# TensorE's semaphore waits placed anew in a single-core cross-attention and gated-adapter kernel

## The chip, the core and the metric

One core of one Trainium2 chip runs the whole kernel. The time is the device time of one execution in microseconds (us); the median of three runs of the kernel before is 473.6 us (472.96 to 475.18). Each engine has its own stream of instructions; they meet only at semaphores. An instruction of this program carries at most one wait of its own. Where the source asks for more, the first stays on the instruction (for a product: on its weight load) and the others go into a separate instruction ahead of it, which the profile shows as EVENT_SEMAPHORE on "PEldq", TensorE's sequencer.

## The reference, cut to what matters

Four sequences of 512 tokens of 1024 features; 64 context rows each.

```
x = x + tanh(g0) * attention(layernorm(x), ctx)
    Q = rmsnorm(text @ Wq.T + bq); K = rmsnorm(rmsnorm(ctx) @ Wk.T + bk)
    attended = softmax(Q @ K.T / sqrt(1024)) @ rmsnorm(ctx)
x = x + tanh(g1) * ffn(layernorm(x))
    base = x @ W_base.T + b_base
    w    = normalised, thresholded softmax gate over 8 experts
    out  = base + 2 * sum_e w_e * (x @ A_e.T) @ B_e.T
```

All of it is float32. The kernel splits an operand into a high and a low part and makes one exact product from three fast ones: high*high, high*low, low*high.

## The kernel before, in words

Each engine's function walks the same list `stages` (lines 355 to 480), written out by hand, and issues what belongs to it; the list is the order of the work.

**First part (to about 240 us).** Q is never formed. With the Gram matrix of Wq (stage `g`) a block of 512 tokens needs only y = G x, in eight column blocks j (stage `y`, lines 674 to 688, one PSUM bank each, three products for each row r in `ROWS[j]`; column block 0 has one row, so three products in all), and its scores s = M x (stage `s`, line 689). VectorE turns each y bank into squares, GpSimd adds them. While block b is in `y`, the block before it is finished: `tops` (transposes of scores, after y(b,0)), `norms` (transposes of the norm sums, after y(b,1)), `pt` (transposes of the probabilities, after s(b)) and `attend` (after y(b,4) to y(b,7), two pairs of products, each emptied by VectorE in line 1465).

**Second part.** Token tiles go in pairs p = 0..7. Pair 0 takes the plain eight 512x128 block products, pairs 1 to 7 seven products P1, P2, P6, P5, P7, P3, P4 (a Winograd scheme; `PRODUCTS`, line 302) over sums of token blocks and of weight blocks (T1 to T4). Each is 12 instructions (lines 769, 771, 773: four k, three high/low products) and adds into PSUM bank A, B, C or D. VectorE adds bank A into the output rows after P1, P6 and P7 and bank C after P5 (stage `part`, line 1534, counted by `v_ev`); P6 may not touch bank A before P1 was read out. In front of the seven come `hd` (the gate and the adapter's A, banks 4 and 5), after P1 and P2 or P6 the one transpose `mt`, after P5 the transposes `zt` a21 and a22 of the next pair, after P7 a11, after P3 a12; `fin` adds the adapter's B. In pair 0 some of this stands elsewhere.

**The ring.** Transposes and `attend` share PSUM banks 7 and 6 in turn. `ring_open` (line 520) gives the next bank and waits until the entry two before it was emptied, by ScalarE (`a_ring`) or VectorE (`v_ring`). `tokens_ready` (line 533) waits for a token block's low part. All of `tensor` (line 519) is in the order of the list, so a wait that isn't met holds everything behind it.

Of the kernel before, what the change touches and what calls it, by code (L numbers as in the profile page):

```python
# [43 lines left out]
def build(nc, x, xt, ctx, front, wq, wk, wb, hd, bt, vec, fn_w, b_base, scal, out):  # L44
    T, D = x.shape
    S_ALL = ctx.shape[0]
    KB = D // P
# [22 lines left out]
    with ExitStack() as stack:  # L70
# [179 lines left out]

        SWEPT = [sorted((min(row, c), max(row, c)) for _, pieces in sweep for row, cols, _ in pieces for c in cols) for sweep in SWEEPS]
# [85 lines left out]
        for p in range(NP):  # L337
            for name, *_ in products(p):
                prod_no[p, name] = len(prod_no) + 1
                if name in PARTS and not plain(p):  # L340
                    ev_no[p, name] = len(ev_no) + 1
            for b_, _, _ in whole(p):
                ev_no[p, b_] = len(ev_no) + 1
        last_use = {op: max(prod_no[p, n] for p in range(NP) for n, _, o, _, _ in products(p) if o == op) for op in w_at}
# [174 lines left out]
        def tensor(pe):  # L519
            def ring_open(key, engine, split=False):  # L520
                n = ring.add(key, engine, split)
                if n >= 2:
                    engine, count = ring.empty(n - 2)
                    pe.wait_ge(ring_sem[engine], count)
                return bank[T_BANKS[n % 2]]
# [21 lines left out]
            for stage, *i in stages:  # L547
# [5 lines left out]
                elif stage == "mr":  # L553
                    b, = i
                    pe.wait_ge(g_mr, b + 1)
                    if b == 0:
                        pe.wait_ge(v_gl, 4)
                    else:
                        pe.wait_ge(v_z, 4 * b)
# [4 lines left out]
                elif stage == "zt":  # L564
# [17 lines left out]
                    acc = ring_open((stage, p, name), "act" if copied else "dve", split=not copied)  # L582
                    pe.wait_ge(a_xn, seq[2 * p + j] + 1)
                    transposes(acc, src)
                elif stage == "mt":
                    t, = i
                    acc = ring_open((stage, t), "dve", split=True)
                    pe.wait_ge(v_mm, t + 1)
                    transposes(acc, mm[t % 2][:, :].unsqueeze(1))
                elif stage == "pt":  # L590
                    b, = i
                    acc = ring_open((stage, b), "act")
# [81 lines left out]
                elif stage == "y":  # L674
# [7 lines left out]
                    pe.wait_ge(v_zl, 4 * b + max(ROWS[j]) // CK + 1)  # L682
                    for r in ROWS[j]:
                        g = block_no(r, j)
                        pe.matmul(acc[:, :], gram[:, g, 0, :], xth[b % 2][:, r, :], start=r == ROWS[j][0], stop=False)  # L685
                        pe.matmul(acc[:, :], gram[:, g, 1, :], xth[b % 2][:, r, :], start=False, stop=False)  # L686
                        done = pe.matmul(acc[:, :], gram[:, g, 0, :], xtl[b % 2][:, r, :], start=False, stop=r == ROWS[j][-1])  # L687
                    done.then_inc(p_y, 1)
                elif stage == "s":
                    b, = i  # L690
                    acc = bank[S_BANKS[b % 2]]
                    pe.wait_ge(v_zl, 4 * b + 4)
                    if b == 0:
                        pe.wait_ge(v_ml, KB)
                    elif b > 1:
                        pe.wait_ge(a_st, b - 1)
                    for r in range(KB):
                        pe.matmul(acc[:, :], mk[:, r, b, :], xth[b % 2][:, r, :], start=r == 0, stop=False)
                        done = pe.matmul(acc[:, :], mk[:, r, b, :], xtl[b % 2][:, r, :], start=False, stop=r == KB - 1)
                    done.then_inc(p_s, 1)  # L700
                elif stage == "norms":
                    b, = i
                    acc = ring_open((stage, b), "dve")
                    pe.wait_ge(g_qsum, qsums(b, FB - 1))
                    transposes(acc, sq_sum[:, :].rearrange("p (j t) -> p j t", j=TPB))
                elif stage == "tops":
                    b, = i
                    acc = ring_open(("weights", b), "dve")
                    pe.wait_ge(a_st, b + 1)
                    transposes(acc, st_sb[:, :].rearrange("p (j t) -> p j t", j=TPB))  # L710
                elif stage == "attend":
                    t, = i
                    b = t // TPB
                    for h in range(NH):
                        acc = ring_open((stage, t, h), "dve")
                        if t % TPB == 0 and h == 0:
                            engine, count = ring.empty(ring.number["pt", b])
                            pe.wait_ge(ring_sem[engine], count)
                            pe.wait_ge(v_fn, b + 1)
                        cols = half(h)  # L720
                        pe.matmul(acc[:, :], pt[b // 3][:, t % TPB, :], fnh[:, cols], start=True, stop=False)
                        pe.matmul(acc[:, :], pt[b // 3][:, t % TPB, :], fnl[:, cols], start=False,
                                  stop=True).then_inc(p_ring, 1)
                elif stage == "hd":
                    p, j = i
                    acc = bank[H_BANKS[j]]
                    if p > 0:
                        pe.wait_ge(v_hg, 2 * p - 1 + j)
                    elif j == 0:
                        pe.wait_ge(v_hw, 3)  # L730
                        pe.wait_ge(v_first, 3)
                    else:
                        pe.wait_ge(a_st, B)
# [4 lines left out]
                    for n, (name, w) in enumerate(uses):  # L738
                        tokens_ready(p, name)
                        z = z_slot[p, name]  # L740
                        for k in range(KH):
                            pe.matmul(acc[:, 0:2 * HEAD], zh[z][:, k, :], hw[w][:, k, :], start=n == k == 0, stop=False,  # L742
                                      skip_group_check=True)
                            done = pe.matmul(acc[:, 0:HEAD], zl[z][:, k, :], hw[w][:, k, 0:HEAD], start=False,  # L744
                                             stop=n == 1 and k == KH - 1, skip_group_check=True)
                    done.then_inc(p_hd, 1)
                elif stage == "prod":
                    p, n = i
                    name, tok, op, n_bank, opens = products(p)[n]
                    if opens and p == 0:  # L750
                        pe.wait_ge(*{"A": (v_dot, NQ - 2), "B": (v_dot, NQ - 1), "C": (v_first, 4), "D": (v_dot, NQ)}[n_bank])
# [5 lines left out]
                    if op in WHOLE_KEPT:  # L757
                        pe.wait_ge(v_wl, SPLITS[op, 1])
                    else:
                        pe.wait_ge(ld_w[op], T_BACK[op])  # L760
                    z = z_slot[p, tok]
                    parts = [(C_BANK[n_bank], 0, HALF)]
                    if (p, name) == (NP - 1, "P4"):
                        parts = spans(p, 3)
                        pe.wait_ge(v_hg, NT - 1)
# [905 lines left out]
```

## Time and profile before

| | |
|---|---|
| median of 3 runs | 473.6 us (472.96 to 475.18) |
| profiled execution: time and span | 473.6 us, with nothing outside the span that matters |
| TensorE products / weight loads, busy | 468.0 us (99%) / 399.3 us (84%) |
| VectorE, ScalarE, GpSimd busy | 361.7 us (76%), 173.8 us (37%), 119.8 us (25%) |
| granted TensorE clock | full in all 40 slices |
| share of the last chain | TensorE 78%, VectorE 8%, DMA 8% |

Products overlap in the pipeline: a 128x512 product shows as 0.39 us long, but the next begins 0.23 us after it. What is to be read is therefore the distance between the starts, not the length. The weight load of a product begins when the product before it begins.

### The profile page before, as it was taken

How to read it: one execution, taken by the hardware profiler on the slowest of the kernel's cores; microseconds unless marked ns; L12 is line 12 of the kernel's file. 1: busy time of each engine (PE TensorE's matmuls, PEld its weight loads, DVE VectorE, ACT ScalarE, POOL GpSimd, SP SyncE). 2: the span in 40 equal slices, each digit the busy share in tenths (PEclk: the TensorE clock that was granted, in tenths of full speed). 3: DMA queues.
4: the chain of work that ended last, by engine and by line, in shares of the span. 5: the costliest groups of instructions: out<-in, count | busy, mean ns of one | idle time of the engine just before them, and what ended most of it. 6: DMA issues, size and time to landing. Idle time of an engine off the chain costs nothing.

```text
span 473.6 us, 6945 instructions
## 1 busy us (share of the span) xinstructions
PE 468.0 (99%) x2481; PEld 399.3 (84%) x2481; DVE 361.7 (76%) x750; ACT 173.8 (37%) x349; POOL 119.8 (25%) x107
## 2 busy tenths in 40 slices
PE   8999999999999999999999999999999999999997
PEld 7898999998887888888888888878888888888886
DVE  1687996588888978879987888968777678877733
ACT  5847532332224305226334625342241421414300
POOL 0020511002344253345242406031230502205000
PEclk9999999999999999999999999999999999999999
DMA  8993129958576378576379640221405032050202
GB/s 320 412 408 118 76 90 389 405 183 286 197 246 248 133 252 283 193 292 229 141 273 419 277 144 36 81 98 46 133 1 175 4 89 90 2 177 1 89 1 89
DMA packets 22114, 84.40 MB, mean 178 GB/s; under 512 B 2624, under 2 KB 3904, under 8 KB 19264
## 3 DMA queue, kind: packets, MB, share of 16 engines
q1 hardware_dynamic: 21792, 83.81, 48.2%
q8 instruction: 20, 0.33, 0.3%
q10 hardware_dynamic: 288, 0.15, 0.1%
q14 instruction: 14, 0.11, 0.1%
HBM read 61.93 MB, written 22.02 MB: 177 GB/s over the span
## 4 chain that ended last, share of the span: by engine, by line
PE 78%; DVE 8%; DMA 8%; issue 3%; ACT 1%; POOL 1%; SPq 0%; DVEq 0%; ACTq 0%
PE bank L769 10%; PE bank L773 10%; PE bank L771 10%; PE bank L649 6%; PE bank L685 5%; PE bank L687 5%; PE bank L686 5%; PE bank L530 4%; PE bank L742 4%; DMA xst<-x_dram 3%; DMA T_low<-t_low_T 2%; DMA xz<-xt_dram 2%; DMA out_dram<-xs 2%; PE bank L599 2%; DVE wl_B L1438 1%
## 5 line engine op out<-in xcount | busy, mean ns | idle before, releaser
L1554 POOL TENSOR_TENSOR small<-small,tiny 128x1 f32<-128x1 f32 (+2 forms) x25 | 23.6, 942 | 167.1 <-DVE small L1183 137.9
L1534 DVE SCALAR_TENSOR_TENSOR xs<-bank,tiny,xs 128x512 f32<-128x512 f32 (+1 forms) x61 | 43.3, 739 | 20.6 <-PE bank L773 14.9
L685 PE MATMUL bank<-xth,gram 128*128 128x512 f32 x144 | 57.3, 398 | 0.0
L687 PE MATMUL bank<-xtl,gram 128*128 128x512 f32 x144 | 56.3, 391 | 0.0
L686 PE MATMUL bank<-xth,gram 128*128 128x512 f32 x144 | 56.1, 390 | 0.0
L769 PE MATMUL bank<-wh_B,zh 128*128 128x512 f32 x116 | 47.0, 405 | 0.1
L769 PE MATMUL bank<-wh_T,zh 128*128 128x512 f32 (+1 forms) x116 | 46.6, 402 | 0.0
L1582 POOL TENSOR_TENSOR sq_sum<-sq_sum,sq 128x512 f32<-128x512 f32 x24 | 32.0, 1333 | 56.5 <-DVE sq L1362 56.5
L773 PE MATMUL bank<-wh_B,zl 128*128 128x512 f32 x116 | 45.6, 393 | 0.0
L771 PE MATMUL bank<-wl_B,zh 128*128 128x512 f32 x116 | 45.4, 391 | 0.0
L773 PE MATMUL bank<-wh_T,zl 128*128 128x512 f32 (+1 forms) x116 | 44.7, 386 | 0.0
L771 PE MATMUL bank<-wl_T,zh 128*128 128x512 f32 (+1 forms) x116 | 44.6, 385 | 0.0
L1614 POOL TENSOR_TENSOR xs<-xs,bb 128x1024 f32<-128x1024 f32 x16 | 39.3, 2461 | 10.3 <-ACT zn L1022 7.7
L1362 DVE SCALAR_TENSOR_TENSOR sq<-bank,gsm,xz 128x512 f32<-128x512 f32 x32 | 23.8, 746 | 14.1 <-PE bank L687 12.6
L979 ACT ACTIVATE xth<-xz 128x1024 fp32r<-128x1024 f32 x16 | 17.0, 1061 | 42.3 <-DVE xz L1258 42.3
L687 PEld LDWEIGHTS bank<-xtl,gram 128*128 128x128 f32 x144 | 27.0, 188 | 5.9
L686 PEld LDWEIGHTS bank<-xth,gram 128*128 128x128 f32 x144 | 27.1, 188 | 5.3
L685 PEld LDWEIGHTS bank<-xth,gram 128*128 128x128 f32 x144 | 27.1, 188 | 5.2
L742 PE MATMUL bank<-hw,zh 128*128 128x276 f32 x128 | 31.1, 334 | 0.0
L744 PE MATMUL bank<-hw,zl 128*128 128x138 f32 x128 | 29.0, 227 | 0.0
L1022 ACT ACTIVATE zn<-xs,small 128x1024 f32<-128x1024 f32 x16 | 19.9, 1242 | 24.1 <-POOL small L1606 24.1
L1047 ACT ACTIVATE zh<-zr 128x512 fp32r<-128x512 f32 x28 | 17.5, 633 | 24.7 <-DVE zr L1298 10.5
(200 smaller groups left out, 1133.2 us busy)
## 6 DMA issues: line engine op xcount, KB each, us to landing
xst<-x_dram SPq DMA_DIRECT2D x16, 512.0 KB, 4.4
xz<-xt_dram SPq DMA_DIRECT2D x16, 512.0 KB, 7.6
out_dram<-xs SPq DMA_DIRECT2D x14, 512.0 KB, 2.7
xa<-x_dram SPq DMA_DIRECT2D x12, 512.0 KB, 3.4
x<-xa SPq DMA_DIRECT2D x12, 512.0 KB, 3.0
xs<-x SPq DMA_DIRECT2D x12, 512.0 KB, 4.0
wq_raw<-wq_dram SPq DMA_DIRECT2D x8, 512.0 KB, 13.8
t_raw_T<-wb_dram SPq DMA_DIRECT2D x4, 1024.0 KB, 16.7
```

The source lines that it names most:

```text
L649: done = pe.matmul(dst, blocks[left][:, row, :], blocks[right][:, cols.start:cols.stop:cols.step, :], start=n == f == left == right == 0, ...
L685: pe.matmul(acc[:, :], gram[:, g, 0, :], xth[b % 2][:, r, :], start=r == ROWS[j][0], stop=False)
L686: pe.matmul(acc[:, :], gram[:, g, 1, :], xth[b % 2][:, r, :], start=False, stop=False)
L687: done = pe.matmul(acc[:, :], gram[:, g, 0, :], xtl[b % 2][:, r, :], start=False, stop=r == ROWS[j][-1])
L742: pe.matmul(acc[:, 0:2 * HEAD], zh[z][:, k, :], hw[w][:, k, :], start=n == k == 0, stop=False, skip_group_check=True)
L744: done = pe.matmul(acc[:, 0:HEAD], zl[z][:, k, :], hw[w][:, k, 0:HEAD], start=False, stop=n == 1 and k == KH - 1, skip_group_check=True)
L769: pe.matmul(acc, zh[z][:, k, :], wh[op][:, k, cols], start=opens and k == 0, stop=False, skip_group_check=True)
L771: pe.matmul(acc, zh[z][:, k, :], wl[op][:, k, cols], start=False, stop=False, skip_group_check=True)
L773: done = pe.matmul(acc, zl[z][:, k, :], wh[op][:, k, cols], start=False, stop=k == KH - 1, skip_group_check=True)
L1534: dve.scalar_tensor_tensor(out=xs[slot][:, cols], in0=bank[n_bank][:, 0:hi - lo], scalar=tg[:, 1:2], in1=xs[slot][:, cols], op0=ALU.mult, ...
L1582: pool.tensor_tensor(sq_sum[:, :], addend[:, :], sq[j % 2][:, :], ALU.add).then_inc(g_qsum, 1)
L1614: pool.tensor_tensor(xs[slot][:, :], xs[slot][:, :], bb[:, :], ALU.add).then_inc(g_x1, 1)
```

## The change

Only `tensor` changes, and two tables that it reads. No product, transpose or instruction of another engine is added or taken out, and the order stays. Waits on semaphores of TensorE are left out, or stand in front of an earlier instruction: one of the last three instructions of the stage in front of the border at which they stood.

```diff
+        ROWS_READY = [...]       # for y(0, j): the v_zl that its rows are the first to need, else 0
+        first_use = {op: ... number of the first product that uses the operand ...}
+            def ring_free(n):
+                engine, count = ring.empty(n - 2)
+                pe.wait_ge(ring_sem[engine], count)
-            def ring_open(key, engine, split=False):
+            def ring_open(key, engine, split=False, known_free=False):
-                if n >= 2: (wait for entry n - 2)
+                if n >= 2 and not known_free: ring_free(n)
 mr:     -  else: pe.wait_ge(v_z, 4 * b)
 zt:     known_free=p > PLAIN and name in ("a21", "a11"); a_xn waited for by a21 and a11 only
 mt:     known_free=p > PLAIN and (p + 1 == NP or 2 * (p + 1) < NT - TPB)
 pt, norms, tops:  known_free=b < B - 1
 y:
-                    pe.wait_ge(v_zl, 4 * b + max(ROWS[j]) // CK + 1)
+                    if b == 0 and ROWS_READY[j]:
+                        pe.wait_ge(v_zl, ROWS_READY[j])
                     for r in ROWS[j]:
                         g = block_no(r, j)
+                        final = r == ROWS[j][-1]
+                        if final and b == j == 0:
+                            pe.wait_ge(v_z, 4)
                         pe.matmul(... gram high, xth ...)
+                        if final and j == 4 and b > 0:
+                            pe.wait_ge(v_fn, b)
                         pe.matmul(... gram low, xth ...)
+                        if final and j < 2 and b > 0:
+                            ring_free(len(ring.emptied_by))
+                        elif final and j == 4 and b > 0:
+                            (wait until pt(b - 1) was emptied)
+                        elif final and j == FB - 1 and b + 1 < B:
+                            pe.wait_ge(v_zl, 4 * (b + 1) + 4)
                         done = pe.matmul(... gram high, xtl ...)
 s:
-                    pe.wait_ge(v_zl, 4 * b + 4)
+                    if b == 0 and 4 not in ROWS_READY[:4]: pe.wait_ge(v_zl, 4)
-                    elif b > 1:
-                        pe.wait_ge(a_st, b - 1)
+                        if r == KB - 1 and b > 0:          # before the last of its products
+                            ring_free(len(ring.emptied_by))
 attend:
-                        if t % TPB == 0 and h == 0:        # waits for pt(b) and v_fn
+                        if t == NT - TPB and h == 0:
 hd:
-                    if p > 0: pe.wait_ge(v_hg, 2 * p - 1 + j)
-                        tokens_ready(p, name)
+                        if j == 0 if p > 0 else (j, n) == (1, 1):
+                            tokens_ready(p, name)
 prod:
-                    elif opens:
+                    elif name == "P1" or name == "P2" and plain(p - 1):
                         pe.wait_ge(v_ev, ev_no[p - 1, n_bank])
-                    elif not plain(p):
-                        pe.wait_ge(v_ev, ev_no[p, {"P6": "P1", "P7": "P6", "P3": "P5"}[name]])
-                    tokens_ready(p, tok)
-                    if op in WHOLE_KEPT: pe.wait_ge(v_wl, SPLITS[op, 1])
-                    else:                pe.wait_ge(ld_w[op], T_BACK[op])
+                    elif name == "P7":
+                        pe.wait_ge(v_ev, ev_no[p, "P6"])
+                    elif name == "P4" and p + 1 < NP:
+                        pe.wait_ge(v_ev, ev_no[p, "P7"])
+                    if name in ("P6", "P3"):
+                        tokens_ready(p, tok)
+                    if first_use[op] == prod_no[p, name]: (the wait for the operand, as before)
                         for k in range(KH):
+                            if k == KH - 1 and name in ("P2", "P7"):
+                                pe.wait_ge(v_ev, ev_no[p, {"P2": "P1", "P7": "P5"}[name]])
                             pe.matmul(... zh, wh ...)
                             pe.matmul(... zh, wl ...)
+                            if k == KH - 1 and name in ("P5", "P7") and 0 < p < NP - 1:
+                                ring_free(len(ring.emptied_by))
                             done = pe.matmul(... zl, wh ...)
 fin:
-                        if p == 0:
+                        if p == n == 0:
                             pe.wait_ge(v_bt, 1)
-                    if n_bank == "A" and not plain(p):
+                    if (p, n_bank) == (NP - 1, "A"):
                         pe.wait_ge(v_ev, ev_no[p, "P7"])
```

In `prod` of pair 0, bank C's wait for `v_first` is left out too, and in the last P4 that for `v_hg`.

## Rows read from the trace of the kernel before

**Rows 1.** The page: busy us, share of the span, count, by engine
```profile
PE 468.0 (99%) x2481; PEld 399.3 (84%) x2481; DVE 361.7 (76%) x750; ACT 173.8 (37%) x349; POOL 119.8 (25%) x107
```
**Rows 2.** Waits of TensorE, who ended them: total us, times, longest us
```profile
PE bank L530 <- DVE px L1394: 0.6, 1, 0.6
...
PE bank L530 <- DVE mtl L1174: 0.2, 1, 0.2
```
**Rows 3.** Separate waits by line: count, ns min/median/max, first and last start
```profile
L758 PEldq EVENT_SEMAPHORE  x36: 51/51/51, 242.4 to 463.1; - x36
...
L696 PEldq EVENT_SEMAPHORE  x2: 51/51/51, 175.3 to 208.8; - x2
```
**Rows 4.** Products at the border y(3,3) to s(3): start, us
```profile
212.39 0.39 PE L686 MATMUL bank<-xth,gram 128*128 128x512 f32 x1
212.62 0.39 PE L687 MATMUL bank<-xtl,gram 128*128 128x512 f32 x1
212.84 0.39 PE L698 MATMUL bank<-xth,mk 128*128 128x512 f32 x1
```
**Rows 5.** y(3,0) and the transposes `tops` behind it, then those of `norms`
```profile
204.56 0.39 PE L686 MATMUL bank<-xth,gram 128*128 128x512 f32 x1
204.78 0.39 PE L687 MATMUL bank<-xtl,gram 128*128 128x512 f32 x1
205.05 0.42 PEld L530 LDWEIGHTS bank<-ident,st_sb 128*128 128x128 f32 x4 [0.31 <-DVE xa L1465]
205.47 0.48 PE L685 MATMUL bank<-xth,gram 128*128 128x512 f32 x1
206.71 0.40 PE L687 MATMUL bank<-xtl,gram 128*128 128x512 f32 x1
207.31 0.47 PE L685 MATMUL bank<-xth,gram 128*128 128x512 f32 x1
```
**Rows 6.** The attend of tile 11: a late weight load
```profile
237.24 1.40 DVE L1465 SCALAR_TENSOR_TENSOR xa<-bank,rt,xa 128x512 f32<-128x512 f32 x2
238.45 0.40 PE L722 MATMUL bank<-fnl,pt 128*128 128x512 f32 x1
238.69 0.19 PEld L721 LDWEIGHTS bank<-fnh,pt 128*128 128x128 f32 x1 [0.29 <-DVE xa L1465]
239.03 0.39 PE L722 MATMUL bank<-fnl,pt 128*128 128x512 f32 x1
```
**Rows 7.** Pair 1: VectorE empties P1, and a product of P2
```profile
280.45 0.75 DVE L1534 SCALAR_TENSOR_TENSOR xs<-bank,tiny,xs 128x512 f32<-128x512 f32 x1
280.77 0.39 PE L773 MATMUL bank<-wh_B,zl 128*128 128x512 f32 x1
```
**Rows 8.** The same in pair 2 and in pair 7
```profile
308.20 0.75 DVE L1534 SCALAR_TENSOR_TENSOR xs<-bank,tiny,xs 128x512 f32<-128x512 f32 x1
308.79 0.40 PE L773 MATMUL bank<-wh_B,zl 128*128 128x512 f32 x1
452.03 0.75 DVE L1534 SCALAR_TENSOR_TENSOR xs<-bank,tiny,xs 128x512 f32<-128x512 f32 x1
452.64 0.40 PE L773 MATMUL bank<-wh_B,zl 128*128 128x512 f32 x1
```
**Rows 9.** Two waits that were not met: pt(0), and B22 in pair 0
```profile
148.60 0.43 DVE L1394 TENSOR_TENSOR px<-pexp,px 128x256 fp32r<-128x256 f32 x1
149.14 0.42 PEld L530 LDWEIGHTS bank<-ident,px 128*128 128x128 f32 x4 [1.03 <-issue]
256.15 1.23 DVE L1438 TENSOR_TENSOR wl_B<-wr_B,wh_B 128x1024 fp32r<-128x1024 f32 x1 [0.23 <-ACT wh_B L1126]
257.49 0.19 PEld L769 LDWEIGHTS bank<-wh_B,zh 128*128 128x128 f32 x1 [0.31 <-issue]
```
**Rows 10.** Pair 2: transposes of a22 behind P5, and VectorE before them
```profile
313.61 1.29 DVE L1178 BATCH_NORM_STATS2 small<-xs 128x6 f32<-128x512 f32 x2 [2.59 <-DMA xs<-x]
316.30 0.66 PE L530 MATMUL bank<-ident,zn 128*128 128x128 f32 x4 [0.24 <-DVE mtl L1174]
```

More of the change, by code:

```diff
@@ L248, in build @@
                                                     for row, cols, _ in pieces for c in cols}] for j in range(KB)]
+        ROWS_READY = [max(ROWS[j]) // CK + 1 if all(max(ROWS[j]) // CK > max(ROWS[i]) // CK for i in range(j)) else 0
+                      for j in range(KB)]
         SWEPT = [sorted((min(row, c), max(row, c)) for _, pieces in sweep for row, cols, _ in pieces for c in cols) for sweep in SWEEPS]
@@ L343, in build @@
                 ev_no[p, b_] = len(ev_no) + 1
+        first_use = {op: min(prod_no[p, n] for p in range(NP) for n, _, o, _, _ in products(p) if o == op) for op in w_at}
         last_use = {op: max(prod_no[p, n] for p in range(NP) for n, _, o, _, _ in products(p) if o == op) for op in w_at}
@@ L519, in tensor @@
         def tensor(pe):
-            def ring_open(key, engine, split=False):
+            def ring_free(n):
+                engine, count = ring.empty(n - 2)
+                pe.wait_ge(ring_sem[engine], count)
+            def ring_open(key, engine, split=False, known_free=False):
                 n = ring.add(key, engine, split)
-                if n >= 2:
-                    engine, count = ring.empty(n - 2)
-                    pe.wait_ge(ring_sem[engine], count)
+                if n >= 2 and not known_free:
+                    ring_free(n)
                 return bank[T_BANKS[n % 2]]
@@ L581, in tensor @@
                     copied = not plain(p) and name == "a21"
-                    acc = ring_open((stage, p, name), "act" if copied else "dve", split=not copied)
-                    pe.wait_ge(a_xn, seq[2 * p + j] + 1)
+                    acc = ring_open((stage, p, name), "act" if copied else "dve", split=not copied,
+                                    known_free=p > PLAIN and name in ("a21", "a11"))
+                    if name in ("a21", "a11"):
+                        pe.wait_ge(a_xn, seq[2 * p + j] + 1)
                     transposes(acc, src)
@@ L586, in tensor @@
                     t, = i
-                    acc = ring_open((stage, t), "dve", split=True)
+                    p = t // 2
+                    acc = ring_open((stage, t), "dve", split=True,
+                                    known_free=p > PLAIN and (p + 1 == NP or 2 * (p + 1) < NT - TPB))
                     pe.wait_ge(v_mm, t + 1)
@@ L591, in tensor @@
                     b, = i
-                    acc = ring_open((stage, b), "act")
+                    acc = ring_open((stage, b), "act", known_free=b < B - 1)
                     pe.wait_ge(v_px, b + 1)
@@ L691, in tensor @@
                     acc = bank[S_BANKS[b % 2]]
-                    pe.wait_ge(v_zl, 4 * b + 4)
+                    if b == 0 and 4 not in ROWS_READY[:4]:
+                        pe.wait_ge(v_zl, 4)
                     if b == 0:
                         pe.wait_ge(v_ml, KB)
-                    elif b > 1:
-                        pe.wait_ge(a_st, b - 1)
                     for r in range(KB):
                         pe.matmul(acc[:, :], mk[:, r, b, :], xth[b % 2][:, r, :], start=r == 0, stop=False)
+                        if r == KB - 1 and b > 0:
+                            ring_free(len(ring.emptied_by))
                         done = pe.matmul(acc[:, :], mk[:, r, b, :], xtl[b % 2][:, r, :], start=False, stop=r == KB - 1)
@@ L702, in tensor @@
                     b, = i
-                    acc = ring_open((stage, b), "dve")
+                    acc = ring_open((stage, b), "dve", known_free=b < B - 1)
                     pe.wait_ge(g_qsum, qsums(b, FB - 1))
@@ L707, in tensor @@
                     b, = i
-                    acc = ring_open(("weights", b), "dve")
+                    acc = ring_open(("weights", b), "dve", known_free=b < B - 1)
                     pe.wait_ge(a_st, b + 1)
@@ L726, in tensor @@
                     acc = bank[H_BANKS[j]]
-                    if p > 0:
-                        pe.wait_ge(v_hg, 2 * p - 1 + j)
-                    elif j == 0:
+                    if p == j == 0:
                         pe.wait_ge(v_hw, 3)
                         pe.wait_ge(v_first, 3)
-                    else:
+                    elif p == 0:
                         pe.wait_ge(a_st, B)
```

17 lines of the change are left out of this document (9 added, 8 removed).

## Prediction, made before the change was built or run

> **What bounds the kernel now.** I read the page's engine rows first: TensorE is busy 468.0 of 473.6 us, VectorE 361.7 [rows 1]. The list of who TensorE waited for then says how much a better placed wait could give at all. It holds five entries, the largest two behind the start being 0.6 us for the transposes of `px` and 0.2 us for VectorE's `mtl` [rows 2]; most waits never hold TensorE. So the kernel is bound by the row of products itself, and a wait can cost in three ways: by the time of its separate instruction, by holding the row when it isn't met, and by its latency when it isn't met. I looked at one place for each.
>
> The separate instruction: each takes 51 ns on TensorE's sequencer; 36 stand at line 758 alone [rows 3], and over all lines I count 189. But they run far ahead. The last one of line 696 belongs to s(3) and starts at 208.8 us, while the first product of s(3) starts at 212.84: 4.0 us ahead [rows 3, 4]. At that border the products start at 212.39, 212.62, 212.84, that is 0.23 and 0.22 us apart, although it has two waits; inside a stage the distance is 0.23 too. A met wait costs nothing that the rows can show (their last digit is 0.01).
>
> **The waits left out.** By the diff about 155 of the 189 separate instructions go. At 0.00 us each [rows 4] the gain is 0. Bounds: 155 x 0.01 = 1.6 us gained at most by the resolution of the rows, and nothing lost, since nothing is added there. I take 0. What hides them is the lead of 4.0 us, about 17 products; with the lead gone (after a wait that held the sequencer) one would cost its 0.05 us.
>
> Two waits that weren't met lose latency, because each is now the only wait of its instruction. In pt(0), `px` is ready at 148.60 + 0.43 = 149.03 and the weight load starts at 149.14, 0.11 later. In pair 0 the low part of B22 is ready at 257.38 and the load starts at 257.49, again 0.11 [rows 9]. Both were separate waits. Where the wait is the load's own it goes faster: VectorE ends at 237.24 + 1.40 = 238.64, the load starts at 238.69, 0.05 later [rows 6]. Gain 2 x 0.06 = 0.12 us.
>
> The sequencer rule is the one that speaks most for a large gain. The Trainium skill (Advanced Engine Details and Errata, Network/Comms) says that reading a semaphore from a sequencer takes 50 to 100 ns. The 51 ns of [rows 3] agree with its lower end. If that time stood on the path, an estimate from the page would give 8 to 16 us; the row on the border shows that it doesn't.
>
> **The waits moved forward.** A wait in front of an earlier product is free only if it is already met there. TensorE loads the weights of a product while the one before it streams, so the wait is asked one product earlier still. What a late load costs I read at the attend of tile 11 [rows 6]: the load comes 0.24 us after the start of the product before it (238.45 to 238.69), and two distances together are 239.03 - 238.45 = 0.58 instead of 0.46. So 0.12 us of lateness is free and the rest is paid. Bounds: none of it free (the cost is the whole lateness) or all of it free up to 0.24.
>
> I went through every moved wait in this way. Most have 0.4 to 10 us in hand. These don't:
>
> *y(2,0) and y(3,0).* `tops` waited for the ring entry that VectorE empties in line 1465; its load starts at 205.05, ended by that [rows 5]. Now the wait is in front of the third (last) product of y(3,0), whose load would follow the second product's start at 204.56. It will start at 205.05 instead, 0.49 late: 0.37 us. The stall was there before, but smaller: from the last product to the first one behind the transposes it is 204.78 to 205.47 = 0.69, and at the met border of `norms` 206.71 to 207.31 = 0.60 [rows 5], so 0.09 goes. Net +0.28, and y(2,0) shows the same distances: together +0.56 us. y(1,0) is safe, its ring entry was emptied long before. Queued behind the wait are the last product, `tops`, and then VectorE's work on both, which has 1 to 2 us in hand.
>
> *P2 of the pairs.* P6 waited until P1 was read out of bank A. Now the wait stands in front of the last three products of P2, 0.7 us earlier. In pair 1 the readout ends at 280.45 + 0.75 = 281.20; with 0.05 the load can start at 281.25; it is wanted at 280.77, with the product before it [rows 7]: 0.48 late, cost 0.36. In pair 7: 452.03 + 0.75 + 0.05 = 452.83 against 452.64, 0.19 late, cost 0.07 [rows 8]; pairs 3 and 4 show the same 0.18 to 0.19, so 0.21 for the three. In pair 2: 308.95 + 0.05 against 308.79, 0.21 late, cost 0.09 [rows 8], but behind it the transposes of a22 start only at 316.30, held by VectorE, whose work goes back to a load from DMA that lets it start at 313.61 [rows 10]. That load doesn't move with TensorE, so the 0.09 only shortens this stall: 0. In pairs 5 and 6 an attend stands between P1 and P2 and the readout is in time. VectorE's readout in turn depends on `hd`, not on P2, so it moves along with the row and takes nothing back.
>
> Met where they now stand: P7's wait for P5's readout, the ring entries asked in P5, P7, y(b,1) and `s`, the `pt` and `v_fn` waits in y(b,4), and `v_zl` of the next block in y(b,7).
>
> **Sum.** 0.56 + 0.36 + 0.21 - 0.12 = +1.0 us on the profiled execution's 473.6, which is also the median of the runs: 474.6 us. With no lateness free the six stalls cost 6 x 0.12 = 0.7 more: 475.3. With the whole 0.24 free, the three of pair 3, 4 and 7 vanish and the others lose 0.12 each: 474.6 - 0.21 - 0.36 = 474.0. The gain of 1.6 us from the waits left out would give 473.0.
>
> **Rivals.**
> 1. *The moved waits are met after all.* The semaphore comes at the time the rows say only within the profile, and 0.1 to 0.5 us earlier would do. Then 473.6 - 0.12 = 473.5. Against it: the load of `tops` is really held until 205.05.
> 2. *Separate waits cost on the path.* 155 x 0.051 = 7.9 us [rows 3] less: 466.7 with the stalls above. For it only the count; against it the 0.22 us at a border with two waits. A weaker form, 20 ns each, is 3.1 us: 471.5. The Trainium skill's figure (Advanced Engine Details and Errata, Network/Comms) points this way too.
> 3. *Slower: P2 held for the whole moved stretch.* If P1's readout comes 0.5 us later than in this profile, the wait in P2 holds for all of the three products by which it moved, 0.69 us, in five pairs (1, 2, 3, 4, 7; pair 2 now beyond what [rows 10] absorb), 3.5 us, with y's 0.56: 477.6. It decides from about 0.5 us; the readout has VectorE's two gates in front of it and VectorE is busy 76%. Against it: the readout is at the same distance from P2 in four pairs, within 0.03 us.
> 4. *The change doesn't do what it says:* waits of one semaphore may fall together in the program, so that fewer go than I count. The time is then that of rival 1 or the forecast, 473.5 to 474.6, since they cost nothing.
>
> **Chances.** A measurement of this kernel tells about 0.5%, 2.4 us, from no change. The forecast 0.58; rival 1 with 4, 0.25; rival 2 in either form 0.10, of which 0.08 is over 0.5% faster; rival 3 0.07, of which 0.05 is over 0.5% slower. So faster 0.09, same 0.86, slower 0.05. The forecast's own range is 474.0 to 475.3, to which the runs' own spread (472.96 to 475.18) adds about 1 us on a side. The range for 8 in 10 reaches to rival 1 and the 1.6 us of the rows' resolution below and some way to rival 3 above: 472.4 to 475.9.
>
> **What would show it.** In y(2,0) and y(3,0): the weight load of line 687's last product about 0.5 us behind the product before it, and `tops` following with no idle time. In P2 of pair 1 a gap in front of the last k of about 0.36 us, and 0.07 in 3, 4 and 7. At the borders with a wait gone: distances of 0.22 to 0.23 as before. pt(0) starts 0.06 nearer to `px`. Under 100 separate waits on TensorE's sequencer. Wrong would be: those loads on time (rival 1), borders that come closer together by 0.02 or more (rival 2), or a hold of 0.5 us or more in P2 of pairs 3, 4 and 7 (rival 3).

## The result, and the profile after

The changed kernel takes 475.31 us (median of 11 runs, 474.33 to 477.2), the kernel before beside it 473.6 (11 runs, 472.43 to 475.18). The ratio is 1.0034, 95% interval 1.0021 to 1.0047: 1.6 us slower (1.0 to 2.2). The interval leaves out no change, but the difference is below the 0.5% that was set as the bound. Leaving out 156 separate waits made the kernel no faster.

The page of the kernel after: busy us, share of the span and count by engine, answering to [rows 1].

```profile
span 475.4 us, 6789 instructions
...
PE 467.8 (98%) x2481; PEld 397.8 (84%) x2481; DVE 361.9 (76%) x750; ACT 173.8 (37%) x349; POOL 120.0 (25%) x107
```

The products are the same and so, within 0.2 us, is their busy time; what is new is idle time. The profiled execution is the one of 477.2 us, so 1.8 us lie outside the span. It is also the slowest of the 11, so this trace shows more than the median has to explain.

Who TensorE waited for in the kernel after (total us, times, longest us), answering to [rows 2]; and the separate waits at line 785, the border of the products, answering to [rows 3]:

```profile
PE bank L797 <- DVE xs L1564: 1.7, 2, 1.3
PE bank L552 <- DVE idle L1215: 1.2, 1, 1.2
PE bank L537 <- DVE px L1424: 1.0, 1, 1.0
```
```profile
L785 PEldq EVENT_SEMAPHORE  x2: 51/51/51, 242.3 to 295.8; - x2
```

The first entry is new. Its two holds are both VectorE's readout of a P product (line 1534 before, 1564 now): one in P2, where the wait was put, one in P7, where it stood before. Over all lines 33 separate waits are left of 189.

The forecast stall in y(3,0), kernel after, answering to [rows 5]:

```profile
204.11 0.39 PE L701 MATMUL bank<-xth,gram 128*128 128x512 f32 x1
204.61 0.19 PEld L709 LDWEIGHTS bank<-xtl,gram 128*128 128x128 f32 x1 [0.54 <-DVE xa L1495]
204.61 0.50 PE L709 MATMUL bank<-xtl,gram 128*128 128x512 f32 x1
204.94 0.60 PE L537 MATMUL bank<-ident,st_sb 128*128 128x128 f32 x4
205.30 0.48 PE L698 MATMUL bank<-xth,gram 128*128 128x512 f32 x1
```

The load was wanted at 204.11 with the product before it and comes at 204.61: 0.50 late. Two distances take 204.94 - 204.11 = 0.83 instead of 0.46, so 0.37 is lost. Over the whole border, 205.30 - 204.11 = 1.19 against 205.47 - 204.56 = 0.91 in [rows 5]: +0.28. The forecast was exact here, and y(2,0) shows +0.29.

Pair 1 of the kernel after, P1's readout and the last three products of P2, answering to [rows 7]:

```profile
280.22 0.39 PE L803 MATMUL bank<-wh_B,zl 128*128 128x512 f32 x1
280.23 0.75 DVE L1564 SCALAR_TENSOR_TENSOR xs<-bank,tiny,xs 128x512 f32<-128x512 f32 x1
281.03 0.19 PEld L797 LDWEIGHTS bank<-wh_B,zh 128*128 128x128 f32 x1 [0.85 <-DVE xs L1564]
281.03 0.50 PE L797 MATMUL bank<-wh_B,zh 128*128 128x512 f32 x1 [0.42 <-DVE xs L1564]
281.37 0.40 PE L799 MATMUL bank<-wl_B,zh 128*128 128x512 f32 x1
```

The load is 281.03 - 280.22 = 0.81 late, not 0.48, and 281.37 - 280.22 - 0.46 = 0.69 us are lost, not 0.36. TensorE is 0.55 us earlier here than in [rows 7] (280.22 against 280.77), the readout only 0.22 (280.23 against 280.45). The pairs 2, 3, 4 and 7 lose 0.09, 0.06, 0.08 and 0.07.

The largest single hold is elsewhere, at P7 of the same pair:

```profile
287.48 1.29 DVE L1208 BATCH_NORM_STATS2 small<-xs 128x6 f32<-128x512 f32 x2 [2.35 <-DMA xs<-x]
...
289.17 0.74 DVE L1564 SCALAR_TENSOR_TENSOR xs<-bank,tiny,xs 128x512 f32<-128x512 f32 x1
...
289.97 0.50 PE L797 MATMUL bank<-wh_T,zh 128*128 128x512 f32 x1 [1.30 <-DVE xs L1564]
```

P7 needs P6's readout. In VectorE's order that readout stands behind the statistics of the next pair, and these wait for a load of x. In the kernel before they start at 285.77, here at 287.48. The DMA queue of SP shows why; first the kernel after, then the one before:

```profile
274.35 0.34 SPq L963 DMA_DIRECT2D out_dram<-xs  x1
278.83 0.32 SPq L952 DMA_DIRECT2D xs<-x  x1
...
284.25 0.32 SPq L952 DMA_DIRECT2D xs<-x  x1
```
```profile
274.57 0.34 SPq L933 DMA_DIRECT2D out_dram<-xs  x1
277.20 0.32 SPq L922 DMA_DIRECT2D xs<-x  x1
...
282.57 0.32 SPq L922 DMA_DIRECT2D xs<-x  x1
```

The load into `xs` is issued when the store in front of it has emptied the buffer: 4.48 us after the store's issue here, 2.63 us in the kernel before. The next store and load queue up behind it; the second load comes 5.4 us after the first in both traces. So the hold of 1.53 us goes back to a slow store, and it is the change's doing only if it comes back.

Taking the two traces product by product: the start and the Gram stage end 1.15 us earlier, pt(0) takes 0.40 more, y(2,0) and y(3,0) 0.57, B22 in pair 0 0.34 less, P2 of pair 1 0.70, P7 of pair 1 1.53, P2 of the other four 0.30, and a22 in pair 2 0.31 less. The sum is +1.70 of the 1.8 by which the spans differ. Of it the moved waits are 0.57 + 0.70 + 0.30 = 1.57, less what a22 took back. The rest is larger in both directions; P7's part of it is followed back to DMA above, the others were not all followed.

### The profile page after: what moved, and what is told of

It is laid out like the page before. It is cut to its first block, busy times and chain, and to the rows that moved or that the text cites. A ratio compares the mean times of both kernels' runs of the same rounds, so it can differ in the third digit from the quotient of the medians.

```text
span 475.4 us, 6789 instructions
## 1 busy us (share of the span) xinstructions
PE 467.8 (98%) x2481; PEld 397.8 (84%) x2481; DVE 361.9 (76%) x750; ACT 173.8 (37%) x349; POOL 120.0 (25%) x107
## 4 chain that ended last, share of the span: by engine, by line
PE 82%; DMA 8%; DVE 6%; issue 2%; ACT 1%; POOL 1%; DVEq 0%; SPq 0%
PE bank L658 11%; PE bank L797 10%; PE bank L803 9%; PE bank L799 9%; PE bank L709 5%; PE bank L698 5%; PE bank L701 5%; PE bank L764 4%; PE bank L537 3%; DMA bt_raw<-bt_dram 3%; DMA out_dram<-xs 2%; DMA xz<-xt_dram 2%; PE bank L680 2%; PE bank L679 2%; PE bank L681 2%
## 5 line engine op out<-in xcount | busy, mean ns | idle before, releaser
L797 PEld LDWEIGHTS bank<-wh_T,zh 128*128 128x128 f32 x116 | 21.8, 188 | 5.9 <-DVE xs L1564 1.5
```

## The experiments

Two theories. **T1:** a met separate wait is paid by TensorE's sequencer, which runs ahead, and only the two moved waits cost, about 1 us. **T2:** something else makes the kernel slower or hides a gain: the slow store, the own waits that took the place of separate ones, or a cost of waits that cancels. Each ratio is to the kernel before on the same chip, with its 95% interval; 1.001 is 0.47 us. For the first four that kernel's median was 473.59, for the next four 473.6, for the runs of three and five waits 473.23, for that of two 474.15. The ratio is not the quotient of the two medians, and the two can differ by about 1 in 1000.

### The changed kernel again

> The changed kernel once more, beside the others. If its 1.6 us over the kernel before are stalls at the moved waits, the trace shows again about 0.28 us each at y(2,0) and y(3,0), 0.4 to 0.7 us in P2 of pair 1 and 0.06 to 0.09 us in P2 of pairs 2, 3, 4 and 7, and a time 1.0 to 1.8 us over the kernel before. The open point is the hold of 1.53 us in front of P7 of pair 1, ended by VectorE, whose work there goes back to a load of xs: if it belongs to the change it stands here again with over 1 us; if it is chance in the DMA it is another size (0 to 2 us), here and in every other kernel of this series.

Measured: 474.88 us (12 runs), 1.0024 (1.0009 to 1.0038), +1.1 us. In its profile P7 of pair 1 is not held, so the 1.53 does not come with the change each time; y(2,0) and y(3,0) cost 0.28 each again, P2 of pairs 2, 3, 4 and 7 costs 0.076, 0.067, 0.071 and 0.068. P2 of pair 1 costs only 0.12 this time:

```profile
279.20 0.75 DVE L1564 SCALAR_TENSOR_TENSOR xs<-bank,tiny,xs 128x512 f32<-128x512 f32 x1
...
279.76 0.39 PE L803 MATMUL bank<-wh_B,zl 128*128 128x512 f32 x1
...
280.00 0.19 PEld L797 LDWEIGHTS bank<-wh_B,zh 128*128 128x128 f32 x1 [0.28 <-DVE xs L1564]
...
280.34 0.39 PE L799 MATMUL bank<-wl_B,zh 128*128 128x512 f32 x1
```

0.24 late, and 280.34 - 279.76 - 0.46 = 0.12 lost. The sum of the moved waits in this execution is 0.56 + 0.12 + 0.28 = 0.96 us.

### Each moved wait put back, and both

```diff
 (P2's wait back at P6)
+                    elif name == "P6":
+                        pe.wait_ge(v_ev, ev_no[p, "P1"])
-                            if k == KH - 1 and name in ("P2", "P7"):
+                            if k == KH - 1 and name == "P7":
                                 ...
 (y's wait back at tops)
-                        if final and j < 2 and b > 0:
+                        if final and j == 1 and b > 0:
-                    acc = ring_open(("weights", b), "dve", known_free=b < B - 1)
+                    acc = ring_open(("weights", b), "dve")
```

> The changed kernel with one part undone: the wait for P1's readout stands in front of P6 again, as before, instead of in front of the last k of P2. Theory (the moved waits hold TensorE): P2 of all pairs runs through, 0.7 + 3 x 0.07 = 0.9 us less than the changed kernel, so +0.6 us over the kernel before, what is left being y(2,0) and y(3,0). Rival (the loss is the 1.5 us at P7 of pair 1, from DMA, and has nothing to do with the moved wait): within 0.3 us of the changed kernel in the mean. Rival (the waits left out cost something through another engine): also no difference.

> The changed kernel with the other part undone: the ring wait of the transposes of the scores (tops) stands at tops again and no longer in front of the last product of y(b,0). Theory: y(2,0) and y(3,0) lose their 0.5 us late weight load, tops gets its small hold of 0.1 us back, 0.56 us less than the changed kernel, +0.5 to +1.0 us over the kernel before. Rival (VectorE's chain behind sets the time there, so that a hold of TensorE at 171 and 205 us is taken back later): no difference.

> The changed kernel with both moved waits back in their places; the 155 separate waits stay left out. Theory (left-out waits cost nothing where they were met, and give 0.06 us at the two places where they weren't): the kernel before, -0.1 to -0.4 us. Rival (separate waits do cost on the path, 20 ns or more each, and the moved waits ate that gain): 3 us or more faster than the kernel before.

| version | separate waits | median us | ratio (95%) | left in its profile |
|---|---|---|---|---|
| changed, again | 33 | 474.88 | 1.0024 (1.0009 to 1.0038) | y +0.56, P2 +0.40 |
| P6's wait back | 39 | 474.47 | 1.0003 (0.9983 to 1.0023) | y +0.56 |
| `tops`' wait back | 36 | 474.57 | 1.0010 (0.9995 to 1.0025) | P2 +0.40 |
| both back | 42 | 474.15 | 1.0008 (0.9992 to 1.0025) | neither |

With P6's wait back, P2 of pair 1 runs through while the readout is under way (it starts at 279.98 and ends at 279.98 + 0.75 = 280.73), and the products keep their old distances:

```profile
280.33 0.39 PE L805 MATMUL bank<-wh_B,zl 128*128 128x512 f32 x1
280.56 0.39 PE L799 MATMUL bank<-wh_B,zh 128*128 128x512 f32 x1
280.79 0.39 PE L801 MATMUL bank<-wl_B,zh 128*128 128x512 f32 x1
281.01 0.40 PE L805 MATMUL bank<-wh_B,zl 128*128 128x512 f32 x1
```

The medians have the order that T1 wants, and 474.88 - 474.15 = 0.7 us lie beside the 0.96 of the profile. The ratios don't have that order (P6's wait back reads lower than both back), and all the intervals overlap. So by time alone neither the two stalls nor these versions are told from each other; by the profiles each stall goes with its own wait. With both back 147 separate waits are gone. A gain of 0.1 to 0.4 us was expected of that; measured is +0.4 (-0.4 to +1.2), no difference that can be told from zero.

### The moved waits alone

The kernel before with all its 189 separate waits, and the two moved ones added in front of their products:

```diff
+                        if r == ROWS[j][-1] and j == 0 and b > 0:
+                            ring_free(len(ring.emptied_by))
+                            if k == KH - 1 and name == "P2":
+                                pe.wait_ge(v_ev, ev_no[p, "P1"])
```

> The kernel before with all its waits, to which only the two early waits are added: the ring wait in front of the last product of y(b,0), b > 0, and the wait for P1's readout in front of the last k of P2. Theory (these two carry the loss, the left-out waits nothing): the same stalls as in the changed kernel, 0.28 us each at y(2,0) and y(3,0), 0.1 to 0.4 us in P2 of pair 1, 0.06 to 0.09 us in pairs 2, 3, 4 and 7, so +0.7 to +1.2 us over the kernel before. Rival (leaving waits out costs time by itself, since the kernel with both waits back read 0.2 to 0.5 us over the kernel before): less than +0.5 us here.

Measured: 475.07, 1.0026 (1.0010 to 1.0043), +1.2 us: all of the loss, with none of the 156 waits taken out. Its profile has y at +0.28 and +0.28, P2 of pair 1 at +0.30 and of 2, 3, 4 and 7 at +0.075, +0.067, +0.070 and +0.068, together 1.14. What settles the cause is these stalls: they stand in every trace that has the moved waits and in none that has them back. The time alone would not, since the run with one further wait per product below reads +1.3 us without any of them.

### P2's wait another three products earlier

```diff
-                            if k == KH - 1 and name in ("P2", "P7"):
+                            if (name, k) in (("P2", KH - 2), ("P7", KH - 1)):
```

> The changed kernel with the wait in P2 another three products earlier (in front of the last two k instead of the last). Theory (every product of 0.23 us by which an unmet wait moves forward is paid in full): 0.69 us more in each of pairs 1, 3, 4 and 7, and in pair 2 as far as the hold at the transposes of a22 doesn't take it back, 2.8 to 3.4 us over the changed kernel; pairs 5 and 6, whose wait has 0.75 us in hand, next to nothing. Rival (VectorE's readout moves earlier or TensorE catches up in what follows): under 1.5 us.

Measured: 477.92, 1.0077 (1.0052 to 1.0101), +3.6 us; between the medians it is 3.0 over the changed kernel, of the 2.8 to 3.4 expected. P2 is now held in all five pairs, and not in 5 and 6. The waits of TensorE in it, and then its pair 2 (the second line is P1's readout):

```profile
PE bank L797 <- DVE xs L1564: 2.5, 5, 0.5
```
```profile
307.92 0.40 PE L803 MATMUL bank<-wh_B,zl 128*128 128x512 f32 x1
308.03 0.75 DVE L1564 SCALAR_TENSOR_TENSOR xs<-bank,tiny,xs 128x512 f32<-128x512 f32 x1
308.83 0.51 PE L797 MATMUL bank<-wh_B,zh 128*128 128x512 f32 x1 [0.51 <-DVE xs L1564]
309.17 0.39 PE L799 MATMUL bank<-wl_B,zh 128*128 128x512 f32 x1
```

0.91 late, 309.17 - 307.92 - 0.46 = 0.79 lost; pairs 1, 3, 4 and 7 lose 0.81, 0.75, 0.77 and 0.77. In pair 2 the stall at a22 gives 0.46 back. Four latenesses of this study, 0.24, 0.50, 0.81 and 0.91, cost 0.12, 0.37, 0.69 and 0.79: each time the lateness less 0.12 or 0.13. The term that the forecast took from one place [rows 6] holds over the whole range.

### VectorE's order, to take out the holds on DMA

From the version with both waits back, the statistics of the next pair behind P6's readout (for P7 of pair 1), and the softmax shares of a block first in y(b,2) (for pt(0)):

```diff
+                if b > 0 and j == 2:
+                    first.append(("shares", b - 1))
 ... (and taken out of its old place, after y(b,2)'s other work)
-                             1: [("attend", t1)] * attends + [("xn", t0), ("stat", t1)],
+                             1: [("attend", t1)] * attends + [("xn", t0)],
+                             2: [("stat", t1)],
```

> The changed kernel with both moved waits back in their places (as e3_both_back) and two steps of VectorE's order changed, by which it no longer stands waiting for a DMA with something behind it that TensorE needs: the shares of block b-1 (px, for the transposes pt) come before the x block that waits for its load from DRAM, and in pairs 1 and up the statistics of the next pair's second tile (which wait for the load of xs) come after P6's readout and not before it. Theory (what is left of TensorE's holds are these two, 0.4 to 1.3 us at pt(0) and 0.3 to 1.5 us at P7 of pair 1 or the transposes of a22 in pair 2, in every profile so far): both holds go, and the time is 1.2 to 2.5 us under the kernel before. Rival (TensorE only meets the next DMA-bound wait sooner): under 0.5 us gained.

Measured: 474.77 (11 runs), 1.0028 (1.0004 to 1.0052), +1.3 us (0.2 to 2.5): no gain, rather the contrary. Both holds are gone in its profile, and another stands behind P7:

```profile
285.16 1.28 DVE L1213 BATCH_NORM_STATS2 small<-xs 128x6 f32<-128x512 f32 x2
...
287.56 1.21 POOL L1641 TENSOR_TENSOR small<-small 128x1 f32<-128x1 f32 x1
...
288.81 1.24 ACT L1057 ACTIVATE zn<-xs,small 128x1024 f32<-128x1024 f32 x1 [2.05 <-POOL small L1641]
...
290.10 0.66 PE L540 MATMUL bank<-ident,zn 128*128 128x128 f32 x4 [1.25 <-ACT zn L1057]
```

From the start of the statistics to the end of `zn` the chain over VectorE, GpSimd and ScalarE takes 290.05 - 285.16 = 4.9 us, and a11 needs its end. The readout no longer waits behind the statistics, but what follows from them does. The wait moved one step on: the transposes of a11 lose 1.41 us against the kernel before. My expectation of a gain of 1.2 to 2.5 us was wrong. Where the +1.3 of the runs comes from stays open; this one profile is of an execution that took 473.95, below the median.

### The price of a met wait

Long-met conditions in front of each of the 1128 products of `y` and `prod`, in the kernel before; slices of 2, 5, 7 and 11 conditions make one, two, three and five further separate waits per product. The first condition stays on the weight load, and a separate instruction carries up to two of the others:

```diff
+            def met():
+                for sem_, v in ((a_ct, 4), (v_ct, 4), (v_kr, 6), (g_const, CONSTS), ...)[:2]:
+                    pe.wait_ge(sem_, v)
+                        met()          # before each of the three matmuls of y and of prod
```

> The kernel before with two long-met conditions added to each of the 1128 products of y and of P1 to P7: one on its own weight load and one as a separate wait on TensorE's sequencer, 1317 separate waits instead of 189. Theory (a met separate wait takes 51 ns of the sequencer, which runs far ahead, and nothing of the path): within 0.5 us of the kernel before. Rival (20 ns or more of each stand on the path): 22 us or more slower; with the full 51 ns, 57 us.

> The same with seven long-met conditions on each of the 1128 products, three further separate waits each. Theory: 3 x 51 = 153 ns of the sequencer plus what a product takes it, which leaves up to 74 ns for that below the 227 ns between two products. If a product takes less than that, the distance stays at 227 and the time at 473 to 476 us; the sequencer's lead over the products is then rebuilt more slowly after each point where it was held, so single borders behind a hold may show up to some 0.1 us. If a product takes more, say 100 ns, the distance is 253 ns and the time some 29 us more. Rival (each met wait costs a fraction of its 51 ns whatever the lead): a tenth of it would be 3384 x 5 ns = 17 us, 491 us.

> The kernel before with eleven long-met conditions on each of the 1128 products of the stages y and prod: five further separate waits each, 5694 more than before in all. By the rows of before each takes 51 ns of TensorE's sequencer. Theory (a met wait is paid by the sequencer alone, and the row pays from the point where the sequencer needs longer for a product than the 227 ns between two of them): the run with one separate wait per product left the distance of the products as it was, so the sequencer needs at most 227 - 51 = 176 ns for a product by itself; with five waits that is 255 ns plus what a product and its weight load take it. Above 227 in any case, so this kernel is slower: by at least 28 ns x 1128 = 32 us, and by (255 + 22 - 227) x 1128 = 56 us if a product takes the sequencer 22 ns. Expected 505 to 550 us, with a distance of 255 to 300 ns in the stages y and prod. Rival (a met wait is free whatever their number): 474 us.

> The same with five long-met conditions on each of the 1128 products, two further separate waits each. The runs with three and five showed distances of 338 and 550 ns, and separate waits that start 106 ns apart, though each is shown as 51 ns long, with 20 ns for the product itself. By that two take 2 x 106 + 20 = 232 ns of the sequencer, against 227 ns between two products. Theory A (only the lead counts: the 5 ns are taken from the sequencer's lead of about 4 us, and the transposes, the gate's products and the adapter's, which have no added waits, give it back): 473 to 476 us, a distance of 227 to 228 ns in most of the row. Theory B (the slower of the two rates holds everywhere): 1128 x 5 ns = 5.6 us more, 479 us, with a distance of 232. The old price of 51 ns would leave 122 ns per product: no change either, so this run tells A from B, not 51 from 106; the two runs before did that.

| further waits per product | median us | ratio (95%) | distance of products |
|---|---|---|---|
| one | 475.17 | 1.0027 (1.0007 to 1.0047) | 0.23 |
| two | 476.44 | 1.0054 (1.0037 to 1.0070) | 0.23 |
| three | 570.39 | 1.2053 (1.2018 to 1.2088) | 0.33 to 0.34 |
| five | 814.73 | 1.7217 (1.7167 to 1.7267) | 0.55 |

Products of P with one, with three and with five further waits, and the separate waits of the run with three:

```profile
439.76 0.39 PE L781 MATMUL bank<-wl_T,zh 128*128 128x512 f32 x1
439.99 0.39 PE L784 MATMUL bank<-wh_T,zl 128*128 128x512 f32 x1
440.22 0.40 PE L778 MATMUL bank<-wh_T,zh 128*128 128x512 f32 x1
```
```profile
440.17 0.47 PE L781 MATMUL bank<-wl_T,zh 128*128 128x512 f32 x1
440.50 0.48 PE L784 MATMUL bank<-wh_T,zl 128*128 128x512 f32 x1
440.84 0.47 PE L778 MATMUL bank<-wh_T,zh 128*128 128x512 f32 x1
```
```profile
440.29 0.47 PE L781 MATMUL bank<-wl_T,zh 128*128 128x512 f32 x1
440.84 0.47 PE L784 MATMUL bank<-wh_T,zl 128*128 128x512 f32 x1
```
```profile
L530 PEldq EVENT_SEMAPHORE  x3526: 51/51/51, 104.4 to 563.7; - x196
```

One further wait leaves the row as it was: from 327 to 453 us of the trace every product starts 0.19 us behind its counterpart in the kernel before, at the end as at the beginning. Its profile has a hold of 1.6 us at `tops` behind a load of `xa`, a place where the trace of the kernel before shows 0.3; whether such chance makes all of its +1.3 us (0.3 to 2.2) was not tried. Three and five cost 97 and 341 us. My expectations for both were far too low, since they took the 51 ns that the row gives as the price. The distances say otherwise: two waits more make 0.55 - 0.34 = 0.21 us, so one is 0.106. In the trace with five, 4352 pairs of consecutive separate waits do start 105 or 106 ns apart, and where a product lies between two of them it is mostly 125 or 126, so a product takes a further 20. Three: 3 x 106 + 20 = 338 ns, five: 550, as measured. Not every product pays this: with three, 309 of 1057 distances inside these stages are still 0.24 us or less. If all 1128 had paid 0.111 us, three waits would have cost 125 us and not 97. The transposes and other products between, which have no added waits, let the sequencer get ahead again; that is argued from the places, not tried.

The run with two was sized by this: 232 ns of the sequencer against 227. The distance stayed at 0.23 through the wide products (229.9 ns in the mean of 976, 229.3 in the kernel before, so some 0.5 us in all). So the lead carries nearly all of the 5 ns, as theory A of that expectation has it, though the median is 0.4 us above its 476. The last P4 has 24 products of 256 columns, though, 0.12 apart in the kernel before. Here, behind the first of them:

```profile
467.08 0.28 PE L784 MATMUL bank<-wh_T,zl 128*128 128x256 f32 x1
467.19 0.28 PE L778 MATMUL bank<-wh_T,zh 128*128 128x256 f32 x1
467.31 0.28 PE L781 MATMUL bank<-wl_T,zh 128*128 128x256 f32 x1
467.44 0.35 PE L784 MATMUL bank<-wh_T,zl 128*128 128x256 f32 x1
467.67 0.36 PE L778 MATMUL bank<-wh_T,zh 128*128 128x256 f32 x1
467.90 0.35 PE L781 MATMUL bank<-wl_T,zh 128*128 128x256 f32 x1
```

At 467.44 the lead is used up and the distance goes from 0.12 to 0.23, for ten products: 1.2 of the 2.6 us that this run lost. Some 0.9 us of it has no place yet. So a met wait does cost time where the sequencer has no lead: up to 106 ns.

The Trainium skill (Advanced Engine Details and Errata, Network/Comms) gives 50 to 100 ns for reading a semaphore from a sequencer. The measured 106 is just past its upper end; the 51 that I had put beside its lower end was not the price.

## Why the prediction was right, and where not

**The size and the sign.** Forecast +1.0 on the median, measured +1.6 (1.0 to 2.2), and in the two repeats +1.1 (0.4 to 1.8) and +1.2 (0.5 to 2.0). The likeliest case was the right one. Part of the agreement is luck, as the two traces are of executions above the medians of their kernels and differ by holds of up to 1.53 us that the prediction doesn't have; what it can claim is the stalls, 0.96 and 1.14 us in the two later profiles.

**The waits left out: 0, right.** With both moved waits back, 147 waits less give 1.0008 (0.9992 to 1.0025); 1128 more leave the distances alone. Rival 2 is out in both its forms: by that interval the 147 gain at most 0.4 us. Its price was mis-sized: 155 x 0.106 = 16.4 us of sequencer time, not 7.9, and still none of it on the path. "With the lead gone one would cost its 0.05 us" was wrong by the same factor. The reason that I gave, the lead of 4.0 us in [rows 3, 4], fits what the runs with two and three waits per product show. [rows 2] I read carelessly: behind the start the second largest entry of that list is 0.3 us for GpSimd's `sq_sum`, not the 0.2 for `mtl`. Nothing hung on it, since the new trace has the same 0.3.

**Latency of an unmet wait.** Right for pt(0): `px` is ready at 147.95 + 0.42 = 148.37, the load starts at 148.42, so 0.05 where it was 0.11. That stage took 0.40 longer all the same, since `px` came later against TensorE. For B22 nothing could be seen: the low part was ready 0.75 us before its load (256.22 against 256.97). The hold of 0.34 us there in the kernel before is in none of the later traces, not even in those that have all its waits. The 0.12 us are below what any of these runs tells.

**y(2,0), y(3,0): right**, +0.28 in every profile that has the wait.

**P2: the mechanism right, one term mis-sized.** Pairs 3, 4 and 7 were forecast at 0.07 each and measured at 0.06 to 0.08. Pair 2 costs 0.08 to 0.09 as said, and a22 gives time back (0.31 here, 0.46 with the wait earlier). Pair 1 was forecast at 0.36 and measured at 0.70, 0.12, 0.11 and 0.30 in four executions. The step that failed is "it moves along with the row". The readout starts before its product by 0.32 us in [rows 7], and by -0.01, 0.56, 0.54 and 0.39 in the four; the load comes 0.80 less that distance late. The traces show what makes it differ. In the changed kernel's first trace VectorE is held here:

```profile
265.81 1.06 ACT L1174 ACTIVATE bth<-bt_raw 128x1024 fp32r<-128x1024 f32 x1 [2.49 <-DMA bt_raw<-bt_dram]
266.91 1.23 DVE L1505 SCALAR_TENSOR_TENSOR btl<-bt_raw,bth 128x1024 fp32r<-128x1024 f32 x1 [0.84 <-ACT bth L1174]
```

In the other three this hold is 0, 0.26 and 0.68 us, in the order of the distances. It goes back to a load from DMA that took 12.2 us to land, against 10.9, 11.3 and 11.8. Up to some 0.6 us of such lateness VectorE makes good at the gate in front of the readout (it waits 0.64 us there for `hl`, against 1.23 in the repeat); what is beyond that, the readout is late. So pair 1 hangs on a load, and one trace gave one draw of it; in hindsight a range of 0.1 to 0.7 would have been right.

**The base.** "The profiled execution's 473.6, which is also the median of the runs" put two different times together. 473.6 is the span of the profiled execution, and in every run since the time is 1.8 us more than the span. So that execution took about 475.4, more than the slowest of the three (475.18), and not 473.6; which one it was isn't on record. The forecast in us came out right because +1.0 was added to the median. Its idle times were also not all typical ones: B22's hold is in no later trace.

**Rivals.** Rival 1, met after all, is refuted by the loads themselves. Rival 3, P2 held for the whole stretch in five pairs, did not come, but pair 1 reached its 0.69 once; with the wait three products earlier it came in all five and at the price that it named. Rival 4 fell: 33 separate waits.

**What the prediction had not.** Holds of 0.3 to 1.6 us (pt(0), `tops`, P7, a22) come and go from one execution to the next, and those that were followed back end at loads from DMA. They are as large as all that this change does. That they make the spread of the runs, some 2 us, is likely but not shown, since each version has one profile.

**What stays open.** How the 0.96 us splits between y and P2 in time, and whether the rest of the first +1.6 is chance. Also why the run with one further wait and the one with VectorE's new order read +1.3 us each, with intervals that leave out 0. No version here beats the kernel before; the one with both waits back can't be told from it.

## What to carry to other kernels

Count a met wait not by its number but by the sequencer's lead: with 512-column products one per product leaves the row alone here and two cost the wide products next to nothing, but a third costs about 0.1 us where the lead is used up. Move a wait forward only if the trace shows its semaphore there before the weight load of the new place, with a margin for the other engine's own drift; what it is late by, less 0.12 us, is lost, and the waits that were replaced here cost 0.09 us (`tops`) and nothing (P6) where they stood. And before a sum is made on a trace, put its span beside its own time and its own time beside the other runs.

## What the runs showed that I had not expected

- A separate wait is shown as 51 ns and takes 106 ns of TensorE's sequencer; a product takes 20 ns more. The start-to-start distance gives the price, the length doesn't.
- The limit is a cliff: two waits per product +0.5%, three +20%, five +72%.
- The five-wait run also shows a lower granted clock, 0.903 over the span against 0.996 with three waits and 1.0 with two: its products stood 0.55 us apart, with idle time between them. The clock is a small part of its 341 us: the median distance is 549 ns where 2.4 GHz was granted and 564 ns where it was 1.2 GHz. Comparing all distances in the stretches at 1.2 GHz with those of the same kind at 2.4 GHz gives an estimate of 15 us.
- The same store took 2.6 us to 4.5 us before its buffer could be loaded again, and in one execution a hold of 1.5 us goes back to it.
